# Cross-attention and a gated mixture on one core: the first half in four phases a batch, with halved turnings, another split of queries and keys, and a late bias

## The reference, cut to what matters

```python
def xattn(v, k, q, mask):                       # q = layernorm(x), v = k = ctx
    qh, kh, vh = heads(q @ wq + bq), heads(k @ wk + bk), heads(v @ wv + bv)
    logits = einsum('bhqd,bhkd->bhqk', qh, kh) / sqrt(16) + mask * -1e9
    out = einsum('bhqk,bhkd->bhqd', softmax(logits), vh)
    return merge(out) @ wo + bo
x = x + tanh(g_xattn[0]) * xattn(ctx, ctx, layernorm(x), mask)
x = x + tanh(g_ffn[0]) * ffn(layernorm(x), ...)  # second half, not touched
```

## Time and profile before

| what | value |
|---|---|
| runs | 1230.52, 1235.73, 1237.83 us; median 1235.73 |
| profiled execution | 1235.98 us, span of its instructions 1234.2 us |
| TensorE busy | 1177.5 us (95%) |
| VectorE, ScalarE, GpSimd busy | 870.7, 643.0, 549.3 us |
| mean granted clock of TensorE | 0.99 of full speed |
| DMA | 200.33 MB, mean 162 GB/s |

### The profile page before, as it was taken

The page is one execution under the profiler, slowest core; times in us unless marked ns, Lnnn a source line. Parts: engine busy times, 40 slices in busy tenths (PEclk is TensorE's granted clock), DMA queues, the critical chain, the costliest instruction groups (busy, mean ns, idle before and its releaser), DMA issues. The chain is left out here.

```text
span 1234.2 us, 42190 instructions
## 1 busy us (share of the span) xinstructions
PE 1177.5 (95%) x16696; PEld 948.8 (77%) x16696; DVE 870.7 (71%) x2492; ACT 643.0 (52%) x1577; POOL 549.3 (45%) x821
## 2 busy tenths in 40 slices
PE   5699999999999999999879999999999999999985
PEld 4477777777777777777658888888888888888874
DVE  3477777777777777777665777677768767777753
ACT  3366666666666666666434444444444444444442
POOL 3476777777677677777610221221222122212110
PEclk9899999999999999999989999999999999999998
DMA  8999999888788778777405777676666757666773
GB/s 226 200 201 201 204 196 198 189 187 179 179 182 182 180 182 184 175 180 161 95 19 120 157 146 162 141 158 142 163 150 144 157 140 157 147 161 148 150 149 96
DMA packets 263012, 200.33 MB, mean 162 GB/s; under 512 B 195934, under 2 KB 243872, under 8 KB 258720
## 3 DMA queue, kind: packets, MB, share of 16 engines
q1 hardware_dynamic: 262816, 197.64, 72.7%
HBM read 125.49 MB, written 72.11 MB: 160 GB/s over the span
## 5 line engine op out<-in xcount | busy, mean ns | idle before, releaser
L899 POOL TENSOR_SCALAR shifted<-raw,neg_max 112x375 f32<-112x375 f32 x512 | 327.2, 648 | 164.4 <-DVE neg_max L781 120.8
L781 DVE CUSTOM_DVE_ANT_0 raw<-bank_s,maskb 112x375 f32<-112x375 f32 x512 | 266.5, 544 | 103.6 <-issue 88.1
L686 ACT ACTIVATE probsT<-bank_t 128x512 f32<-128x512 f32 (+3 forms) x512 | 189.1, 458 | 104.8 <-PE bank_t L460 104.8
L447 PE MATMUL bank_s<-K_stack,Q_stack 128*112 128x375 bf16 x512 | 150.8, 335 | 5.0 <-DVE neg_max L781 4.7
L460 PEld LDWEIGHTS bank_t<-ident,shifted 48*128 48x128 f32 (+1 forms) x3072 | 105.6, 139 | 28.1 <-issue 25.0
L460 PE MATMUL bank_t<-ident,shifted 48*128 48x48 f32 (+1 forms) x3072 | 122.8, 226 | 0.3 <-issue 0.3
L203 POOL TENSOR_SCALAR var_eps<-moments 112x1 f32<-112x1 f32 x32 | 7.2, 225 | 255.4 <-DVE moments L199 255.3
L1167 PE MATMUL bank_ab<-xnT,wq2T 128*128 128x224 f32 x512 | 109.5, 357 | 1.4 <-ACT kT L1383 0.6
L1167 PE MATMUL bank_ab<-xnT,wk2T 128*128 128x224 f32 x512 | 109.5, 357 | 0.0
L482 PE MATMUL bank_o<-probsT,V 128*32 128x112 f32 x3072 | 100.6, 263 | 5.0 <-ACT probsT L686 5.0
L1167 PEld LDWEIGHTS bank_ab<-xnT,wq2T 128*128 128x128 f32 x512 | 94.2, 190 | 12.3 <-issue 7.4
(11 more groups left out here) (149 smaller groups left out, 2237.0 us busy)
## 6 DMA issues: line engine op xcount, KB each, us to landing
K_stack<-k_dram SPq DMA_DIRECT2D x64, 562.5 KB, 7.5
k_dram<-k_parts SPq DMA_DIRECT2D x32, 562.5 KB, 4.7
att_dram<-att_q SPq DMA_DIRECT2D x31, 511.0 KB, 3.3
att_th<-att_dram SPq DMA_DIRECT2D x31, 511.0 KB, 4.4
v_dram<-mv SPq DMA_DIRECT2D x32, 455.0 KB, 7.2
v<-v_dram SPq DMA_DIRECT2D x32, 455.0 KB, 4.5
K_stack<-k_dram SPq DMA_DIRECT2D x32, 375.0 KB, 9.3
Q_stack<-q_dram SPq DMA_DIRECT2D x64, 168.0 KB, 9.2
```

What stands on the lines that cost most here:

```text
L447: nc.tensor.matmul(bank_s[h % 2][0:S, 0:S2], Q_stack[:, p, h, :], K_stack[:, p, h, :], start=True, stop=True).then_inc(scores_ready, 1)
L686: act.activation(probsT[:, g % 2, first_u:end, lo:hi], bank_t[0:KP, bank, column:column + (end - first_u) * (hi - lo)].rearrange("p (u q) ...
L781: dve.tensor_tensor_reduce(raw[:, g % 2, j, :], bank_s[h % 2][0:S, 0:S2], c.maskb[:, :], -1.0, -LEAST, ALU.add, ALU.min, neg_max[:, g % 2, ...
L899: pool.tensor_scalar(shifted[:, g % 2, j, 0:S2], raw[:, g % 2, j, :], -1.0, neg_max[:, g % 2, j:j + 1], ALU.mult, ALU.add).then_inc(shift_ ...
```

## The change

All of it is in the first half.
- **Four phases.** The bodies now begin with score 4 and end with group 2 of the next stage. A phase is four scores with some filling, one turning of the group whose scores are complete, and one weighing of the group before it: phase 1 scores 4 to 7, turns group 0, weighs group 3 of b-1; phase 2 scores 8 to 11, turns 1, weighs 0; phase 3 scores 12 to 15, turns 2, weighs 1; phase 4 scores 0 to 3 of b+1, turns 3, weighs 2. The context and x are turned for b+3, at the end of phase 4, behind each other.
- **Halved turning.** Context, x, heads and the normalised heads are turned in two halves of 64 partitions, which write two banks (`turn_halves`). xn and heads are padded to 128 partitions. The halves of ctxT and xnT are copied by ScalarE (half 0) and VectorE (half 1). The channel order of the heads changes, so wo is loaded in four pieces.
- **Split.** ScalarE writes only the first bf16 part. VectorE makes the rest straight from PSUM (bias added, part subtracted, `key_rest` for each half t, `query_rest`), GpSimd the third part of the keys in halves. The scale of 1/4 is in wq. x is normalised ahead of the query rest.
- **Waits.** `heads_back` waits on the rests of both key halves and of the queries, the second half of the keys on the rest of the first, the first keys on both copies of ctxT and xnT.
- **Transfers.** Queries are stored in three parts, not five, ahead of the keys; they are loaded by four transfers, not three. x is loaded a batch at a time.
- **Bias.** `add_bias` stands at the end of GpSimd's batch.

```diff
-Q_COPIES = 5
-STACKED = ((0, 3, 1), (3, 3, 2), (6, 2, 0))
+K_STACKED = ((0, 3, 0), (3, 3, 0), (6, 2, 0))
+Q_STACKED = ((0, 1, 2), (1, 2, 0), (3, 2, 0), (5, 3, 0))
...
+            def turn_halves(columns, width, src, f):
+                for r in range(2):
+                    rows = slice(r * HALF, (r + 1) * HALF)
+                    last = nc.tensor.transpose(bank_ab[0:f.stop - f.start, r, columns:columns + width], src[rows, f], c.ident[rows, rows])
+                return last
...
+            def body(b):
+                S_(b, 4, 5)
+                if b + 2 < B:
+                    keys(b + 2, 0, 0)
+                S_(b, 6)
+                if b + 2 < B:
+                    queries(b + 2)
+                elif b + 2 == B:
+                    open_gates(0)
+                S_(b, 7)
+                turn(b, 0, b == 0)
+                if back:
+                    weigh(b - 1, 1 - p, NG - 1, False)
+
+                S_(b, 8, 9)
+                if b + 2 < B:
+                    keys(b + 2, 1, 0)
+                S_(b, 10, 11)
+                turn(b, 1, b == 0)
+                if back:
+                    if b + 2 < B:
+                        pe.wait_ge(k_rest_done, EC * (b + 3))
+                        pe.wait_ge(q_rest_done, EC * (b + 3))
...
+                    heads_back(b - 1)
+                weigh(b, p, 0, b == 0)
+
+                S_(b, 12, 13)
...
+                        pe.wait_ge(heads_done, b)
...
+                    values(1 - p, 0)
+                    values(1 - p, 1).then_inc(va_ready, 1)
+                S_(b, 14, 15)
+                turn(b, 2, False)
+                if back:
+                    if b + 1 < B:
+                        pe.wait_ge(v_copied, 2 * b + 3)
+                    heads_turn(b - 1)
+                weigh(b, p, 1, False)
+
+                S_(b + 1, 0, 1)
...
+                    values(1 - p, 2).then_inc(vb_ready, 1)
...
+                S_(b + 1, 2)
+                if back:
+                    project(b - 1)
+                S_(b + 1, 3)
+                if b + 1 == B:
+                    open_proj(1)
+                turn(b, 3, False)
+                if b + 3 < B:
+                    turn_ctx(b + 3)
+                    turn_x(b + 3)
...
+                weigh(b, p, 2, False)
...
+            def key_rest(b, p, t, bank):
+                dve.wait_ge(k_copied, EC * b + t + 1)
...
+                dve.scalar_tensor_tensor(k_rest[:, t, :], bank_ab[:, bank, 0:S2], c.bk[:, t:t + 1], k_parts[:, p, 0, t, :],
+                                         ALU.add, ALU.subtract).then_inc(k_rest_done, 1)
...
+                score_max(b, b == 0, 7)
+                if x_next < 0:
+                    normalise_x(b + 3)
...
+                if b + 2 < B:
+                    query_rest(b + 2)
+                score_max(b, b == 0, 8, 9)
+                if b + 2 < B:
+                    split_rest(b + 2)
+                score_max(b, b == 0, 10)
+                if b + 2 < B:
+                    key_rest(b + 2, p, 1, 0)
+                score_max(b, b == 0, 11)
+                if back:
+                    normalise(b - 1)
...
+                if back:
+                    residual(b - 1)
+                if b + 1 < B:
+                    score_max(b + 1, False, 3)
+                if b + 3 < B:
+                    ctx_copy(b + 3)
+                    x_copy(b + 3)
```

More of the change, by code:

```diff
@@ L529, in open_proj @@
                 last.then_inc(o.proj_ready, 1)
-            def body(b, p, i, first, ahead, last):
-                back, front = not first, not last
-                S_ = lambda *hs: [scores(b, p, i, h, first) for h in hs]
-                if ahead:
-                    transposes(b + 2, i + 1, p)
-                S_(0, 1)
-                if back:
-                    weigh(b - 1, 1 - p, NG - 2, False)
-                    turn(b - 1, NG - 1, False)
-                S_(2, 3)
-                if ahead:
-                    keys(b + 2, p, 0)
-                S_(4)
+            def body(b):
+                p = b % 2
+                back = b > 0
+                S_ = lambda n, *hs: [scores(n, n % 2, n // 2, h, n == 0) for h in hs if n < B]
+                S_(b, 4, 5)
[8 more added lines that the diff above has]
+                turn(b, 0, b == 0)
@@ L628, in _ @@
             pe.wait_ge(v_copied, 2)
-            batches(pe, body)
-            weigh(B - 1, 1, NG - 2, False)
-            open_proj(0)
-            turn(B - 1, NG - 1, False)
+            for h in range(G):
+                scores(0, 0, 0, h, True)
+            for b in range(B):
+                body(b)
             weigh(B - 1, 1, NG - 1, False)
-            pe.wait_ge(o.xt_copied, 2)
+            pe.wait_ge(x_done, B - 1)
             heads_back(B - 1)
-            open_proj(1)
             heads_turn(B - 1)
@@ L666, in query_copy, with key_copy @@
+            def key_copy(b, t, bank):
+                act.wait_ge(k_ready, EC * b + t + 1)
+                if t == 0 and b > 1:
+                    act.wait_ge(k_stored[b % 2], 16 * (b // 2))
+                act.activation(k_parts[:, b % 2, 0, t, :], bank_ab[:, bank, 0:S2], ACT.Identity, bias=c.bk[:, t:t + 1]).then_inc(k_copied, 1)
+            def query_copy(b):
                 act.wait_ge(q_ready, b + 1)
-                if not (isinstance(b, int) and b == 0):
+                if b > 0:
@@ L869, in _ @@
             last_rank.then_inc(o.consts_done, 1)
+            dve.wait_ge(tails_set, 1)
             moments_of(0)
             normalise_x(0)
+            ctx_copy(0)
+            for t in range(EC):
+                key_rest(0, 0, t, t)
             dve.wait_ge(v_set, 1)
@@ L949, in _ @@
                     last_set.then_inc(v_set, 1)
-                key_rest(b, b)
+                for t in range(EC):
+                    key_third(b, b, t)
                 add_bias(b)
-            batches(pool, body)
+            inverse_deviation(2)
+            add_bias(2)
+            shift(0, 0, True)
+            for b in range(B):
+                body(b)
 def switch(nc, z, d, c):
```

484 lines of the change are left out of this document (245 added, 239 removed).

## The result

The changed kernel takes 1241.92 us (median; 1237.79 to 1245.87, seven executions), the kernel before 1235.25 (eight, 1230.52 to 1237.83): ratio 1.0056, 95% interval [1.0034, 1.0078]. It is slower by about half a per cent, at the edge of what can be told from no change. The forecast was 1233, 2.4 us faster than the profiled execution before; the sign came out the other way. (One more execution took 2841.6 us and is left out as disturbed.)

A forecast was written before the change was run, and what follows sets the result against it. TensorE, busy 99.97 of 100 us, was taken to bound the kernel. +2.3 us over 29 batches and -4.7 at the ends made -2.4 against the profiled 1235.98: 1233 us, range 1213 to 1247.

The forecast's parts named there:

- first score: Start of the kernel: queries stored first, keys about 2 us later, loads queued behind; +1.4 us, bounds 0 and 3.
- first score to the end of batch 0: Opening: four scores alone, two loops, 2.3 us; then batch 0, 15.4 plus 1.4 at the low clock, 16.8 us.
- batch 31 and what follows: End of the first half: last batch 16.0 us (14 to 18), then 8.3 from its last turning to the second half.
- both ends together: Stretches outside the 29 full batches: 59.8 against 65.9 us, with the later start -4.7 (bounds -9 and 0).
- TensorE's work: Per batch on TensorE: halved turnings save 0.54 us, scores in fewer places 0.08; 18.07 becomes 17.45 us.
- Its rival on this: Halved turnings on TensorE run fully in parallel, a pair at 0.059, 0.24 us more saved a batch: 1226.5; chance 0.05.
- The wait: Phase 2, before the heads' turning: TensorE's 2.94 us from score 8 against VectorE's 3.66, about 0.7 us once a batch.
- the wait is not there: Rival, phase 2: the 0.7 us shrinks to 0.3 or towards 0; period 17.5 to 17.8, 1211 to 1223 us; chance 0.22.
- The first keys: Keys of the next context: half copies take 1.0 to 1.1 us under a cover of 1.08; taken at 0.
- the slow rival: Half copies of context and x end behind their cover, first keys wait 0.4 us a batch: +11.6, 1245; chance 0.2.
- a first score later than 48 us: Opening: one of the listed signs that would show the forecast wrong; the first score was at 45.03 us before.
- The first rival: Phase 2: if VectorE's cast and key rest run short, the 0.7 us before the heads' turning shrinks; centre 1218, chance 0.22.

The follow-up runs named there:

- experiment 9: Changed kernel with each context turned twice into the same place, six more pairs of halves a batch: 1257.51 us, 1.0177 of the kernel before.
- Experiment 2: Changed kernel with the second key rest one place later on VectorE, behind maximum 11: 1258.71 us, 1.0198 of the kernel before.
- experiment 1: Changed kernel with the queries' cast and subtraction moved on VectorE behind the division of the heads: 1234.33 us, 0.9999 of the kernel before.
- experiment 11: Changed kernel with group 0 weighed ahead of the heads' turning and of the waits for the rests: 1243.88 us, 1.0064 of the kernel before.
- experiment 6: Changed kernel with the queries' cast behind the division of the heads and their subtraction behind maximum 13: 1232.62 us, 0.9971 of the kernel before.
- experiment 12: Experiment 6 with context 0 copied first, keys stored first and the second half's two projections moved: 1222.62 us, 0.9913 of the kernel before.
- experiment 8: Experiment 3 with the keys stored ahead of the queries: 1237.74 us, 1.0019 of the kernel before.
- experiment 3: Changed kernel with VectorE's half copy of context 0 first in its opening: 1237.34 us, 1.0033 of the kernel before.
- experiment 5: Experiment 4 with GpSimd's subtraction for the first key half moved behind the shifts of group 2: 1236.95 us, 1.0032 of the kernel before.
- experiment 4: Changed kernel with the query rests ahead of the normalising of x on VectorE: 1252.32 us, 1.0146 of the kernel before.
- experiment 10: Changed kernel with group 0 weighed ahead of the heads' turning, the waits for the rests staying in front of both: 1261.88 us, 1.0231.

## Why the prediction was right or wrong

The forecast put the second half's start at 637.17 - 2.4 = 634.8 us; it came at 641.19, 6.4 later:

| term | forecast | measured | difference |
|---|---|---|---|
| first score | +1.4 (46.4) | +4.2 (49.23) | +2.8 |
| first score to the end of batch 0 | 2.3 + 16.8 = 19.1 | 70.72 - 49.23 = 21.5 | +2.4 |
| batches 1 to 29 | 526.2 + 2.3 = 528.5 | 529.8 | +1.2 |
| batch 30 | 16.4 | 16.2 (600.48 to 616.68) | -0.2 |
| batch 31 and what follows | 16.0 + 8.3 = 24.3 | 24.5 (to 641.19) | +0.2 |

The second half came out 0.2 us shorter, 596.8 for the 597.0 that the forecast left as it was, and with that the profiled execution stands 6.3 us over the forecast.

**What made the sign.** The forecast had both ends together give 4.7 us and the batches cost 2.3. The ends cost 0.5 (4.2 later at the first score, 3.7 given back), and the batches cost 3.5. Two terms of the opening, the start and batch 0, hold 5.2 of the 6.4 us.

**TensorE's work: right in sum.** 18.18 less the wait of 0.74 and 0.07 ahead of the first keys is 17.37; the forecast had 17.45. Its parts differ: six pairs of the context take 0.39, two of x 0.21, four of headsT 0.36, two of heads 0.23, together 1.19 against the forecast's 1.05; but a group's turning that is followed by halved tiles takes 0.78 instead of 0.89, twice a batch (ahead of the heads and of the context), which gives 0.22 back: 0.97. In batch 30, where nothing is waited for, the heads' turning too follows the group's turning by 0.79 (606.39, 607.18). Counted by that, TensorE's own work is 17.26 and the wait is 0.85: the sum of the two, which the forecast had as 18.15, is surer than its parts. A further pair costs 0.063 (experiment 9), against 0.118 for an old tile, 1.9 times. That is nearer to the factor of up to 2 in the Trainium skill, "TensorEngine Tiling (Array Packing)", Theoretical Speedup, than the 1.6 that the forecast took from the probability turnings; over all 14 pairs it is 1.59 to 0.97, 1.6 again. Its rival on this lost for another reason: pairs of x and headsT cost more than a context pair, and the start took more than it gave.

**The wait: right, in place, size and releaser.** Forecast 0.7, measured 0.74; 3.66 against 3.68 in the chain, though single terms were off by up to 0.12 in both directions, and that they cancel so well is luck. The largest is the queries' subtraction, 0.58 from start to start for 0.46: it took 0.39 where GpSimd rested and takes 0.65 beside a shift here. Experiment 2 shows the wait on the path at full price, and experiment 1 that 0.46 of it goes when two instructions are moved away. That none is given back later held too. What the forecast did not see is the second chain right behind: its rival "the wait is not there" gave 17.5 to 17.8 from the first chain alone (and so 1215 to 1223 us; the 1211 written there does not follow, nor does the 0.24 of the rival behind it, which is 14 x 0.016 = 0.22). Experiments 1 and 11 take the wait away, all or most of it, and get 18.0 and 18.09, since the maxima 12 and 13 or the divided heads are late next. Only with the whole of VectorE's work between score 8 and maximum 13 rearranged (experiments 6 and 12) does the period reach 17.7.

**The first keys: 0.07**, in the bounds of 0 and 0.4. Keys at 308.52 take 1.33 to the next score, 1.26 elsewhere; they start in time, and the profile names no releaser for the 0.07. So the slow rival (half copies behind their cover, 0.4 a batch, 1245) was not what happened, although the time came out near its.

**The start: the step that failed.** "Queries are stored first and the keys about 2 us later ... start +1.4 (bounds 0 and 3)". It counted SyncE's order alone, and that it did roughly: about 1 us, 1.2 in experiment 8 against experiment 3. It left out VectorE's opening list, in which the new half copy of context 0 stands behind an operation that waits for x from DRAM and one that waits for GpSimd: 2.9 us in experiment 3, or 2.2 against the mean of all kernels with that list. In the kernel before ScalarE made the whole copy and nothing of x stood in front of it:

```profile
14.69 4.25 PE L414 MATMUL bank_ab<-ctxT,wk_sb 128*128 128x375 f32 x8 [0.90 <-ACT ctxT L646]
```

These first keys came at 14.69; the changed kernel has them at 17.02, experiment 3 at 13.11. The forecast had named a first score later than 48 us as a sign that it is wrong.

**Batch 0: the second miss**, 2.4 us. The forecast added "1.4 at the low clock that this stretch has now", a figure for which it showed no row. Granted clock (column before the last two) of stretches around the first score, before:

```profile
44.00:47.00 3.00, 2.55 (x10) 1.63 (x9) 1.02 (x4) 0.81 (x1) 0.55 (x1) 0.50 0.73 111
47.00:49.00 2.00, 2.00 (x5) 1.14 (x5) 1.59 (x6) 0.00 (x0) 1.33 (x4) 0.65 1.17 234
49.00:53.00 4.00, 2.99 (x29) 1.78 (x28) 2.50 (x10) 1.86 (x4) 3.06 (x6) 1.00 0.99 201
```

And in the changed kernel:

```profile
48.00:53.00 5.00, 3.96 (x23) 2.24 (x24) 3.01 (x11) 0.66 (x2) 2.07 (x4) 0.50 0.59 134
53.00:57.00 4.00, 4.00 (x13) 2.73 (x12) 2.27 (x9) 0.58 (x1) 2.52 (x6) 0.50 0.94 189
57.00:60.00 3.00, 3.00 (x34) 2.17 (x34) 2.32 (x11) 2.48 (x7) 1.84 (x4) 0.96 0.97 218
```

From its first turning there TensorE runs at 1.2 GHz (0.50) for about 9 us (48.19 to 57) instead of under 5 (43.73 to 48.4, by the 0.65 of 47 to 49), with the new four scores in loops of 1.44 and 1.32 us in front of the work. It had stood 5.3 us ahead of that turning (6.8 before). Why it stayed at the lower level longer no run here isolates; what it cost can be read. The keys take 2.50 instead of 1.26, the queries 1.64 instead of 0.88, the pair of scores ahead of them 0.82 instead of 0.37 and the loops 0.5 more than the 1.12 each that was counted: 2.95 us for the 1.4. A wait of 0.38 for maximum 11 comes to it; some 0.5 us I cannot place.

**Batches 1 to 29.** The undisturbed period, 18.18, is within the forecast's 18.0 to 18.3; 0.03 over 18.15 makes 0.9 of the 1.2 us. The rest is single stalls: 6 of 28 batches are 0.14 to 1.14 us over the undisturbed period, and every kernel here has some, the one before too (2.2 us in all against 2.5), at varying places. The largest, batch 27, is VectorE's normalising beside GpSimd's subtraction (experiment 5). **Batches 30, 31 and the end** were right to 0.2 us each, and the second half did not change.

**Cast and GpSimd.** The first rival's argument was that the cast might run short. It took 0.51 where the chain needs it. The Trainium skill, "GPSIMD Engine Reference", Specifications, says that GpSimd shares its SBUF interfaces with VectorE, with contention when VectorE runs in a 2-port mode or has two SBUF inputs. The trace agrees for the queries' subtraction, which has two (0.39 alone, 0.65 beside a shift). The cast and the normalising have one tensor from SBUF, and no trace shows in which mode they ran; they pay as well. Experiments 4 and 5 show the price by itself, and it is much higher beside GpSimd's subtraction of two tensors than beside its shifts of one.

**What stays open.** The medians lie 6.7 us apart, the profiled executions 3.9. The changed kernel's runs spread over 8 us; the profiled one is among its shorter ones. I take the single stalls for the reason, but no trace of a long run was taken. The late bias, x loaded a batch at a time and the four loads of the queries were not tried singly; between 70 and 600 us the trace of the changed kernel names no transfer as a releaser of TensorE.

## What to carry to other kernels

When a change cuts an engine's work and ties it by one new wait to another engine, sum both chains from the last point that they share, and then the next chain behind the wait as well: taking the wait away is worth only the distance to that second one (in experiment 11 0.19 of 0.74 us, of which 0.09 reached the period). Before moving an instruction within a list that has idle time, look what GpSimd does in the new place; the same place in the list cost 0.46 us a batch more with a GpSimd subtraction beside it than without, 29 x 0.46 = 13 us in all (experiments 4 and 5). In an opening, put the work on the path in front of anything that waits for a transfer, since an in-order list makes the copy wait for data it does not need.

## What the runs showed of the hardware

- VectorE's normalising (112x256, fp32, two scalars) took 0.42 us in the opening, 0.53 beside a shift in the changed kernel, and 1.43 beside GpSimd's subtraction of two 128x375 tensors (0.85 us there). The cast of 128x224 to bf16: 0.28, 0.51 beside shifts, 1.00 to 1.06 beside the subtraction. Beside the subtraction VectorE's operation ends 0.13 or 0.14 us behind GpSimd's in the rows of experiments 1 and 4, although it had started first; beside shifts it ends while GpSimd still shifts (the cast at 296.51, the two shifts at 296.96).
- VectorE's operations with their large input in PSUM did not change: the division of the heads (112x256) took 0.42 beside the subtraction in experiment 10 (306.21, GpSimd from 305.86 for 0.90) and 0.42 beside a shift in the changed kernel (299.01). The key rest has means of 64 between 601 and 605 ns in all kernels, but it stood beside shifts and small operations, beside the subtraction only once, in the opening (0.61).
- A turning by two halves of 64 partitions into two banks costs 0.063 to 0.065 us where many follow each other, but 0.09 to 0.12 where only two or four do; and what follows a group's turning starts 0.78 to 0.79 behind it instead of 0.89 when it is a further halved turning.
